# Linear-attention layers: the four gelus of the feed-forward in one group, projection quarters 0 and 1 joined, the second norm in the projection's bank

## The reference

```python
Q  = elu(x @ Wq + bq) + 1                 # 16 heads of 64: 1024 columns
Kf = elu(x @ Wk + bk) + 1
V  = x @ Wv + bv
KV, sumK = sum_s(Kf * V), sum_s(Kf)       # per sequence, column by column
att = Q * KV / (Q * sumK + 1e-6)
y = gelu(att @ Wo + bo)
x = layer_norm(y + x) * ln1_s + ln1_b
h = gelu(x @ W1 + b1)                     # 512 columns
h = gelu(h @ W2 + b2)
x = layer_norm(h + x) * ln2_s + ln2_b
```

## Time and profile before

| | before |
|---|---|
| median of 3 runs | 3323.68 us (3323.03 to 3341.3) |
| profiled execution | 3324.58 us, span 3322.8 us |
| granted TensorE clock, mean | 0.957 of full speed |
| the stack of layers, about | from 823 us to 3178 us of the span |

### The profile page before, as it was taken

One profiled execution on the slowest core, in us unless ns is written; L12 is line 12 of the kernel. 1 busy time (PEld: TensorE's weight loads), 2 busy tenths in 40 slices (PEclk: granted clock), 3 DMA queues, 4 the chain that ended last, 5 costly groups with the idle time before them and its releaser, 6 DMA issues. The chain is left out here.

```text
span 3322.8 us, 49526 instructions
## 1 busy us (share of the span) xinstructions
PE 3011.6 (91%) x14486; PEld 1989.9 (60%) x14486; DVE 2777.8 (84%) x11011; ACT 2463.9 (74%) x4579; POOL 589.9 (18%) x715
## 2 busy tenths in 40 slices
PE   7999998282799999999999999999999999999779
PEld 5777776271566566566666656666665665666454
DVE  6878786864689999998999998999989999898566
ACT  6878786132578878878888888888888888878535
POOL 0000001276011111111111111111211111111124
PEclk9999998585999999999999999999999999999869
DMA  1000000323000000000000000000000000000000
GB/s 55 1 1 1 0 1 4 110 39 90 1 1 1 7 26 1 3 31 1 1 7 26 1 4 29 1 1 7 26 1 7 26 1 1 7 11 1 1 1 26
DMA packets 35120, 46.39 MB, mean 14 GB/s; under 512 B 5768, under 2 KB 26304, under 8 KB 34880
## 3 DMA queue, kind: packets, MB, share of 16 engines
q1 hardware_dynamic: 29248, 39.47, 3.6%
q0 software_dynamic: 5632, 4.20, 1.0%
HBM read 35.16 MB, written 8.49 MB: 13 GB/s over the span
## 5 line engine op out<-in xcount | busy, mean ns | idle before, releaser
L1880 DVE TENSOR_SCALAR t_feat_q<-t_recip,t_neg_mean 128x256 f32<-128x256 f32 x1024 | 385.5, 438 | 131.4 <-ACT t_recip L1723 131.4
L1554 PE MATMUL t_o_ps<-t_feat_q,t_wo 128*128 128x512 f32 x1024 | 473.0, 595 | 2.7 <-DVE t_feat_q L1880 2.7
L1715 ACT ACTIVATE t_recip<-t_feat_q,t_z_scale 128x256 f32<-128x256 f32 x1024 | 434.7, 498 | 3.5 <-DVE t_feat_q L1880 2.7
L1701 ACT ACTIVATE t_exp_k<-t_k_ps 128x1024 f32<-128x1024 f32 x256 | 259.4, 1013 | 230.2 <-PE t_k_ps L1528 230.2
L1843 DVE CUSTOM_DVE_ANT_0 t_junk<-t_v_ps,t_feat_k 128x256 f32<-128x256 f32 x1024 | 390.3, 418 | 6.1 <-PE t_v_ps L1528 6.0
L1833 DVE SCALAR_TENSOR_TENSOR t_feat_k<-t_exp_k,t_k_ps 128x256 f32<-128x256 f32 x1024 | 368.7, 415 | 21.4 <-ACT t_exp_k L1701 21.4
L1705 ACT ACTIVATE t_exp_q<-t_q_ps 128x1024 f32<-128x1024 f32 x256 | 261.7, 1022 | 96.8 <-PE t_q_ps L1528 94.5
L1869 DVE SCALAR_TENSOR_TENSOR t_feat_q<-t_exp_q,t_q_ps 128x1024 f32<-128x1024 f32 x256 | 312.5, 1221 | 8.8
L2008 POOL TENSOR_TENSOR t_var_eps<-t_moments,t_ln_eps 128x4 f32<-128x4 f32 x128 | 69.2, 540 | 1300.1 <-DVE t_moments L1891 1300.1
L1554 PEld LDWEIGHTS t_o_ps<-t_feat_q,t_wo 128*128 128x128 f32 x1024 | 194.3, 190 | 175.4 <-issue 154.5
L1526 PE MATMUL t_v_ps<-t_x_hi,t_w_hi 128*128 128x512 f32 x512 | 264.4, 516 | 10.1 <-DVE t_sum_kv L1843 9.3
(11 more groups left out here) (365 smaller groups left out, 7341.2 us busy)
## 6 DMA issues: line engine op xcount, KB each, us to landing
t_raw_w<-in_wq SPq DMA_DIRECT2D x8, 512.0 KB, 3.7
t_raw_w<-in_wk SPq DMA_DIRECT2D x8, 512.0 KB, 4.8
t_raw_w<-in_wv SPq DMA_DIRECT2D x8, 512.0 KB, 5.6
t_wo<-in_wo SPq DMA_DIRECT2D x32, 128.0 KB, 2.2
x<-in_x SPq DMA_DIRECT2D x4, 512.0 KB, 8.4
tokens_dram<-r_hn SPq DMA_DIRECT2D x8, 256.0 KB, 2.3
e_w_raw<-in_fc_w SPq DMA_DIRECT2D x4, 512.0 KB, 4.0
e_w<-in_fc_w SPq DMA_DIRECT2D x4, 512.0 KB, 4.9
```

The lines of the kernel that those rows point to most:

```text
L1554: last = pe.matmul(o_ps[:], wo[:, chunk, :], feat_q[:, s, chunk, :], start=(chunk == 0), stop=(chunk == NC - 1), skip_group_check=True)
L1701: act.activation(exp_k[:], k_ps[:], ACT.Exp, bias=-1.0).then_inc(c["k_exp"], 1)
L1715: last = act.activation(recip[:, q % 2, k * UNIT + n * SEQ:k * UNIT + (n + 1) * SEQ], feat_q[:, s, chunk, cols], ACT.Ln, bias=1.0, scale=z ...
L1880: last = dve.tensor_scalar(feat_q[:, s, chunk, cols], recip[:, q % 2, k * UNIT + n * SEQ:k * UNIT + (n + 1) * SEQ], -1.0, neg_mean[:, s, n ...
```

## The change

The gelus of hidden blocks 2 and 3 follow that of block 1 directly on ScalarE, and the return to the ln/exp table between the two groups goes, so that a step has one stay in the gelu table. TensorE's order follows: feed-forward blocks 2 and 3 are issued earlier, around the keys of quarter 1. Projection quarter 0 moves from the middle of the step before to the start of the next step, ahead of quarter 1 and behind the turning of the first norm, which is now the first thing in a step. The second norm uses the projection's bank `o_ps` instead of `m0`; so the second feed-forward no longer waits for the written state, projection quarter 0 does, and the second norm's first turning waits for the gelu that empties `o_ps`.

```diff
 def project(u, s, q):
                 if q == 0:
                     pe.wait_ge(c["y1_ready"], u + 1)
+                    if u >= 3:
+                        pe.wait_ge(c["state_t_ready"], u - 3 + 2 + PER)
...
-            def second_feed_forward(u, follows):
+            def second_feed_forward(u):
...
-                if follows:
-                    pe.wait_ge(c["state_t_ready"], u - 1 + 2 + PER)
...
 TensorE, step
-                if C:
-                    project(t - 2, s, 1)
                 if Dn:
                     pe.wait_ge(c["n1_ready"], 4 * (t - 3) + 5)
                     turn(m1, y1, c["n1_turned"])
+                if C:
+                    project(t - 2, s, 0)
+                    project(t - 2, s, 1)
...
                     values(t, s, 0, 0)
-                    keys(t, s, 1)
-                    queries(t, s, 1)
                 if Dn:
                     first_feed_forward(t - 3, 2)
                 if A:
-                    values(t, s, 0, 1)
+                    keys(t, s, 1)
                 if Dn:
                     first_feed_forward(t - 3, 3)
-                if B:
-                    project(t - 1, r, 0)
+                if A:
+                    queries(t, s, 1)
+                    values(t, s, 0, 1)
                 if E:
                     pe.wait_ge(c["z2_ready"], t - 4 + 2)
-                    if Dn:
-                        pe.wait_ge(c["hid_ready"], 4 * (t - 3) + 5)
-                    turn(m0, y2, c["z2_turned"])
+                    pe.wait_ge(c["y1_ready"], min(t - 2, UNITS - 1) + 2)
+                    turn(o_ps, y2, c["z2_turned"])
...
-                    turn(m0, y2, c["n2_turned"])
+                    turn(o_ps, y2, c["n2_turned"])
...
 ScalarE, step
                     first_gelu(t - 3, 1)
+                    first_gelu(t - 3, 2)
+                    first_gelu(t - 3, 3)
                 if A or B:
                     act.preload_act_table_set("natural_log_exp_and_others")
                 if B:
                     exp_z(t - 1, 0)
                 if A:
                     exp_keys(t, 1)
                     exp_queries(t, 1)
...
-                if Dn:
-                    first_gelu(t - 3, 2)
-                    first_gelu(t - 3, 3)
-                if A or B:
-                    act.preload_act_table_set("natural_log_exp_and_others")
                 if B:
                     log_z(t - 1, r, 1)
                     exp_z(t - 1, 1)
...
 ScalarE's written state, VectorE's statistics and normalisation of the second norm: m0 becomes o_ps
```

More of the change, by code:

```diff
@@ L1660, in step @@
                 if Dn:
-                    second_feed_forward(t - 3, E)
+                    second_feed_forward(t - 3)
                 if A:
@@ L1784, in step @@
                     act.wait_ge(c["n2_turned"], t - 4 + 2)
-                    act.activation(g["state_t"][:, bass.ds(place_of(t - 4), 1), :], m0[:].unsqueeze(1), ACT.Identity,
+                    act.activation(g["state_t"][:, bass.ds(place_of(t - 4), 1), :], o_ps[:].unsqueeze(1), ACT.Identity,
                                    bias=param(t - 4, 9), scale=param(t - 4, 8)).then_inc(c["state_t_ready"], 1)
@@ L1959, in step @@
                 if E:
-                    layernorm_stats(t - 4, 1, m0, c["z2_turned"], c["bn2_done"], c["stats2_ready"])
+                    layernorm_stats(t - 4, 1, o_ps, c["z2_turned"], c["bn2_done"], c["stats2_ready"])
                 if C:
@@ L1967, in step @@
                 if E:
-                    normalise(t - 4, 1, m0, y2, c["rstd2_ready"], c["n2_ready"])
+                    normalise(t - 4, 1, o_ps, y2, c["rstd2_ready"], c["n2_ready"])
                 if C:
```

## The result

The changed kernel took 3664.01 us (median of 4 runs, 3662.47 to 3667.15) against 3323.36 us for the kernel before: a ratio of 1.100 with a 95% interval of 1.097 to 1.104, so 340 us slower. The forecast was 3625 us.

The account below looks back on a forecast made before the run. TensorE was taken to set the pace, at 35.08 us a step. A step of 40.2 us, 5.1 more, over 61 steps gives 311; 3324.6 + 311 − 8 = 3628, stated as 3625 us, range 3545 to 3700 (chance 0.74).

Parts of the forecast that it names:

- The gelus in one group: ScalarE's gelus 2 and 3 ahead of three exps: TensorE's bias matmuls of quarter 2 start 3.36 us later.
- b+6.15: Predicted start of the exp of Z 0, in us after b, the start of quarter 1's bias matmuls; b+2.10 before.
- The second gap on TensorE: Idle time on TensorE between the value block and the bias matmuls of quarter 2, about 1 us a step.
- The table loads: Two ScalarE table switches go, 2.57 us a step, worth nothing on the path because ScalarE has 5.85 us idle.
- faster: Rival: without the loads ahead of Z 1 and the written state, TensorE's waits go, about 3250 us; chance 0.06.
- The rest of TensorE's loop: TensorE from biases 2 to the next biases 1: 25.0 us of work plus 1.58 of projection quarter 0, 26.6.
- The second norm's wait: New TensorE wait of 0.69 us ahead of the second norm's turning back, swallowed if TensorE is late itself.
- TensorE's clock: Clock falls in TensorE's gap each step: cost between 0 and 3.02 us, one slow stretch (1.51) taken, partly inside the gap.
- the clock costs more: Rival: two slow stretches a step on TensorE, a loop of 42.1 us, about 3750 us; chance 0.10.
- The draining: In the four draining steps at the end, waits go: about −8 us, bounds −12 and 0.
- The layer ends: Steps with weight swaps on ScalarE and VectorE, 36.70 us before; their surcharge was taken as unchanged.
- The joined projection: Projection quarter 0 moved into TensorE's stretch after biases 2: four matmuls, 1.58 us.

Follow-up runs that it names:

- Experiments 1 and 2: 1: changed kernel with ScalarE's old list alone put back, 3380.15 us; 2: kernel before with ScalarE's list alone changed, 3705.28 us.
- experiment 5: Changed kernel with the exp of Z 0 alone moved ahead of the gelus and the table load: 3636.21 us, 1.093 of before.
- experiment 4: Changed kernel with 15 extra matmuls of constants in TensorE's gap in each inner step: 3603.5 us, 1.083 of before.
- experiment 3: Changed kernel with ScalarE's list and the place of feed-forward blocks 2 and 3 put back, keeping joined projection and shared bank: 3341.56 us, 1.005 of before.

## Why the prediction was right, and where it was off

The direction, the mechanism and nearly every point of time held.

- *The gelus in one group.* Predicted: exp of Z 0 at b+6.15, attention 0 at b+7.31, features done at b+12.37, biases 2 at b+12.5. Measured: 6.12, 7.29, 12.34, 12.50. Experiments 1 and 2 show that this list is the cause of most of the loss; experiment 5 shows that it does not hang on the first of the three exps alone. The second gap on TensorE, put at about 1 us, is 0.31, because the value block ahead of it ran at the low clock (it is 0.98 in experiment 4 where the clock holds).
- *The table loads* were worth nothing, as predicted: 169 us less ScalarE work and 340 us more time. The rival "faster" was the Trainium skill's rule to group activations by table set ("ScalarE: Activation LUTs", "Table sets: the hidden batching unit"); here the grouping put gelus that wait for TensorE ahead of exps that did not have to.
- *The rest of TensorE's loop.* From the second norm's turning back to the next biases 1 it is 2316.53 to 2339.36, 22.83 us; the prediction's pieces give 26.6 − 3.67 = 22.9.
- *The second norm's wait* was swallowed by a late TensorE, as allowed for; where the clock holds it returns (experiment 4).
- *TensorE's clock is the step that was mis-sized.* From biases 2 to the turning back TensorE needed 5.73 us (2310.80 to 2316.53) instead of 3.67 of work: 2.06 us, where I put in 1.1 net (40.2 less 39.1). I took one slow stretch as long as that in the earlier trace rows, 3.38 us, and argued that half of it is spent inside the gap. In the changed kernel the slow matmuls run for 6.5 us (2308.83 to 2315.34), and only the first 2 us, the value block and the short wait, lie ahead of the biases. In length that is the rival "the clock costs more"; its 42.1 us a step were not reached. The step of 41.06 lies above the 39.8 to 40.6 that I gave for it, and just under the 41.2 that the upper end of the range stands for. The Trainium skill ("TensorE: Matmul & The Clock Gate", "What's actually happening") has the low level as the default that activity releases; the trace agrees, 0.50 behind 3.91 us of idleness. Experiment 4 gives the price from the other side, 1.4 us a step where the clock holds (41.0 to 39.6).
- *The draining* gave 13 us, just outside my bounds of 0 to 12. *The layer ends* I took as unchanged. Before the change they add 4.5 us a layer to eight inner steps, after it about 3 (331.1 less eight of 41.0); that part of the weight swaps falls into the new waits is my guess, which no run shows. The layer ends and the 5 us of draining beyond my 8 took back some 20 of the 50 us by which 59 steps of 41.06 instead of 40.2 exceed the forecast. That the sum came closer than the step is luck.
- *The joined projection* I costed only through its matmuls. By experiment 3 it costs 17 us even with the old list, because projection 0 no longer fills the time in which TensorE would wait for the query features. I also missed the wait of attention 3, 1.99 us there and 2.10 in the changed kernel; TensorE shows no wait that follows from it.

Two things are not settled. The cause of the 17 us of experiment 3 is read from its trace; no run gave projection 0 alone its old place back. And no run shows why the clock falls in some steps of experiments 1 and 4 and not in others with the same gaps.

## What to carry to other kernels

On engines that work through lists in a fixed order, price a merge of two groups by what the moved instructions wait for, not by what it saves: an instruction that waits for another engine makes all behind it wait, and work saved on an engine that is idle at times anyway, 169 us here, need not be worth anything. Follow the delayed instruction through the engines to the next place where the bounding engine stops, and add what that engine's clock loses behind the stop. Undoing one list and applying that list alone are two cheap runs that settle such a question.

## What the runs showed of the hardware

A TensorE gap of 3.91 us in each step, and a short one behind it, cost 2.06 us of slower matmuls after them (0.425 instead of 0.233 us from start to start, granted clock 0.50), and 15 matmuls of constants in the gap made the kernel 60 us faster. Gaps of 0.67 and 0.98 us still let the clock fall in some steps and not in others (mean 0.96 and 1.00 in the two stretches of experiment 4), and so did gaps of 0.43 and 0.99 us in experiment 1 (0.95 in the step from 2161.16 to 2198.17, 1.00 in the one before it). In experiment 3, with 0.98 and 0.41 us, the two inner steps from 2104.20 to 2175.41 had a granted clock of 1.00. A load of an activation table took 1.28 us, and the next activation, where it did not wait for another engine, started 1.29 or 1.30 us behind the load's start in the steps shown.
